# Expert tiles of 128 rows, all expert weights resident in SBUF, results in two regions by tile parity

## The chip, the cores and the metric

The kernel runs on one core of one Trainium2 chip. The metric is device time in microseconds (us) of one execution, lower is better; a version's time is the median of its runs. A core has TensorE (PE, matmuls; its weight loads are shown as PEld), VectorE (DVE), ScalarE (ACT), GpSimd (POOL), SyncE (SP) and 16 DMA engines, which work side by side and wait for each other through semaphores. All tensors are float32.

## What is computed

Gated cross attention of 32 batches of 100 tokens over 1444 context rows, followed by a feed-forward part with 12 experts, of which each token uses three. Cut to what matters:

```
x = x + tanh(g_xattn) * attention(layernorm(x), ctx)          # 32 x 100 x 256
h = layernorm(x); logits = h @ Wr + br                        # 12 experts
top_vals, top_idx = top_k(softmax(logits), 3); ew = softmax(top_vals)
for e in range(12):
    sel = top_idx == e; mask = sel.any(-1); w_e = sum(ew where sel) / max(sel.sum(), 1)
    y = relu(h @ w1[e] + b1[e]) @ w2[e] + b2[e]               # 256 -> 640 -> 256
    out = out + mask * (w_e * y)
phi = sigmoid(relu(mean_tokens(out) @ Wp1 + bp1) @ Wp2 + bp2)
x = x + tanh(g_ffn) * out * (1 - 0.8 * (phi > 0.7))
```

So 9,600 pairs of a token and an expert go through an expert.

## The kernel before

The program has two blocks. The first, `attention`, takes some 1,760 us. It also routes: at the end of each batch POOL scatters the 100 normalised rows three times into the DRAM tensor `rows_by_expert` (`xs`), which has a region for each expert; a row there carries 256 values and, for each expert, the number of the row of `results_by_token` (`ys`) to which its result is to be added. When the last batch is done DVE makes a table in SBUF: for each tile its expert, its first row in `xs`, and the column of the weight. At the same time `clear_pads` on SP and ACT (L295) zeroes one tile's worth of rows behind each expert's last row, 12 DMAs, and SP waits for them (L400). During the last batch ACT issues one DMA that clears `ys` (L592).

The second block, `experts`, is what the change is about. `RT` is the rows of a tile, 256. The number of tiles is fixed: `TILES = (9600 + 12 * (RT - 1)) // RT` = 49. They are in order of expert, and tiles behind the last expert work on zeros. The matmuls of a tile of 256 rows are, each done as two passes, so two instructions in the profile:

- `transpose_x` (L1405): four transposes of the rows `x_t` into `xT_ps`.
- `h_ps` (L1424): 5 chunks of 128 hidden values, 2 matmuls each with a 128x128 piece of w1 as stationary operand and the tile's rows (`xT`, 256 columns) as the moving one: 20 instructions.
- `y_ps` (L1438): for each half of 128 rows 5 matmuls, the hidden values `hid` stationary and w2 (256 columns) moving: 20 instructions.

PE goes h of tile t, transposes of t+1, y of t-1. ACT does five Relu with the bias from PSUM to `hid` (L1300), then copies the next `xT` (L1285), then reads the expert's number from the table and loads the next b2, broadcast over the partitions (L1280). DVE works out the rows of the results (`places`, L1347 and L1353), multiplies b2 by the expert's weight (L1367) and, for each half, evicts `y_ps * weight + b2_w` to `y_t` (L1374). POOL scatters each half into `ys` with an indirect DMA that adds in DRAM (L1211). Rows without a token go to spare rows of their own. Because a token can be in tiles of three experts, POOL starts tile t only when tile t-1 has landed (`y_stored`); the two halves of a tile belong to one expert and are in flight together.

SP loads for every tile: the rows, four tiles deep (L1230), and w1, b1 and w2 of its expert, two tiles deep (L1238, L1242, L1246), 1.31 MB a tile whether or not the expert is the one of the tile before. Each reads the table first. A load into a buffer waits until that buffer's matmuls are done.

After the last tile SP reads `ys` back in 5 pieces of 640 KB (L1269). DVE adds rows within each piece (L1381, L1384), PE sums them by batch (L1449, L1453), a small chain gives the factor, and DVE and SP finish and store the output.

The rule that POOL follows:

```
if t > 1:
    pool.wait_ge(y_stored[(t - 2) % OUT], 16 * RB * ((t - 2) // OUT + 1))
for r in range(RB):
    pool.wait_ge(y_read, RB * (t - 1) + r + 1)
    pool.indirect_dma_start(
...
```

## Time and profile before

| | us |
|---|---|
| median of 3 runs | 2262.12 (2259.59 to 2262.18) |
| profiled execution | 2268.39 |
| its span | 2266.4 |
| PE busy | 2145.9 (95%) |
| DVE busy | 1411.2 (62%) |
| ACT busy | 1160.2 (51%) |
| POOL busy | 805.1 (36%) |
| mean DMA rate | 152 GB/s |

The span is the time between the first and the last recorded instruction; 2.0 us of the execution lie outside it. Busy time counts instructions of an engine, without its register, semaphore and DMA-issuing instructions. Times in the rows count from the start of the span. A matmul's record is longer than the distance to the next one, since matmuls overlap in the array: distances between starts tell the pace. "Landing" is the time from a DMA's issue to the last byte's receipt.

### The profile page before, as it was taken

The page shows a single profiled execution, that of the slowest core. Times are in us where ns is not written, and L with a number is a line of the kernel's source. Part 1 is how long each engine was busy: PE and PEld are TensorE (multiplying, and loading weights), DVE is VectorE, ACT ScalarE, POOL GpSimd, SP SyncE. Part 2 cuts the span into 40 slices and gives each one's busy share as a digit, 9 for nine tenths or more (in the row PEclk, how much of TensorE's full clock was granted, in tenths as well). Part 3 has the DMA queues.
Part 4 walks back from the last instruction along what each step waited for, and adds up shares of the span by engine and source line. Part 5 has one row for each costly group of instructions (what it writes and reads, how often), then busy time and mean ns, then how long its engine had stood idle before and what let it go on. Part 6 is the DMA issues. An engine that isn't in the chain of part 4 may idle for free. (4 is left out here: it accounts for less than half of the span.)

```text
span 2266.4 us, 61917 instructions
## 1 busy us (share of the span) xinstructions
PE 2145.9 (95%) x23554; PEld 1870.7 (83%) x23554; DVE 1411.2 (62%) x3223; ACT 1160.2 (51%) x2765; POOL 805.1 (36%) x1199
## 2 busy tenths in 40 slices
PE   5899999999999999999999999999995789999995
PEld 4688888888888888888888888888874678888884
DVE  4777777777777777777777777777763111111113
ACT  1366666666666666666566656666653223333331
POOL 4323433343344334333433443343311233333331
PEclk9999999999999999999999999999996899999997
DMA  5555555555555555555555555555532786887775
GB/s 135 148 137 148 137 137 140 134 136 144 137 133 134 139 143 140 139 140 134 134 143 137 136 133 137 148 136 139 130 107 58 207 266 187 221 222 218 213 213 169
DMA packets 253828, 345.07 MB, mean 152 GB/s; under 512 B 90296, under 2 KB 170652, under 8 KB 253404
## 3 DMA queue, kind: packets, MB, share of 16 engines
q1 hardware_dynamic: 221228, 303.28, 50.0%
q0 software_dynamic: 20256, 23.21, 5.4%
q10 hardware_dynamic: 12048, 14.63, 2.1%
q8 instruction: 186, 3.05, 0.6%
q14 instruction: 110, 0.90, 0.1%
HBM read 155.83 MB, written 42.86 MB: 88 GB/s over the span
## 5 line engine op out<-in xcount | busy, mean ns | idle before, releaser
L637 DVE TENSOR_REDUCE max_part<-max_ps 100x1 f32<-100x512 f32 (+1 forms) x1536 | 993.9, 655 | 355.1 <-PE max_ps L925 326.8
L513 ACT ACTIVATE probs<-score_ps 128x400 f32<-128x400 f32 x1498 | 733.4, 503 | 411.6 <-PE score_ps L908 402.9
L925 PE MATMUL max_ps<-k_stack,q_stack 96*100 96x512 f32 (+1 forms) x1536 | 597.4, 389 | 15.4 <-DVE max_part L637 14.9
L908 PE MATMUL score_ps<-q_stack,k_stack 97*128 97x200 f32 (+1 forms) x2996 | 599.2, 282 | 0.9
L908 PEld LDWEIGHTS score_ps<-q_stack,k_stack 97*128 97x128 f32 (+1 forms) x2996 | 464.2, 184 | 66.1 <-issue 30.4
L442 POOL TENSOR_TENSOR ctx_hi<-ctx_raw,zero_col 128x256 fp32r<-128x256 f32 (+1 forms) x384 | 213.6, 589 | 467.1 <-PE v_ps L939 433.7
L976 PE MATMUL pv_ps<-probs,v_ones 128*17 128x100 f32 x12288 | 304.9, 251 | 5.5 <-ACT pv_out L521 2.8
L976 PEld LDWEIGHTS pv_ps<-probs,v_ones 128*17 128x17 f32 x12288 | 257.5, 98 | 51.8 <-issue 39.0
L925 PEld LDWEIGHTS max_ps<-k_stack,q_stack 96*100 96x100 f32 x1536 | 257.2, 167 | 28.2 <-DVE max_part L637 23.6
L1300 ACT ACTIVATE hid<-h_ps,b_c 128x256 f32<-128x256 f32 x245 | 116.2, 474 | 311.0 <-PE h_ps L1424 305.2
L1211 POOL DMA_INDIRECT results_by_token<-y_t,slot x98 | 152.6, 1557 | 317.5 <-DVE y_t L1374 183.3
L447 POOL TENSOR_TENSOR ctx_lo<-ctx_raw,ctx_hi 128x256 fp32r<-128x256 f32 (+1 forms) x384 | 257.7, 703 | 7.5
L1374 DVE SCALAR_TENSOR_TENSOR y_t<-y_ps,wexp,b_w 128x256 f32<-128x256 f32 x98 | 47.4, 484 | 318.6 <-PE y_ps L1438 318.6
L562 ACT ACTIVATE k_hl<-k_ps,bk_c 128x512 fp32r<-128x512 f32 (+1 forms) x192 | 127.2, 663 | 221.0 <-PE k_ps L956 196.6
L1424 PE MATMUL h_ps<-xT,w_raw 128*128 128x256 f32 x980 | 225.3, 386 | 10.9 <-DMA w_raw<-in_w 9.9
L939 PE MATMUL v_ps<-w_hi,ctx_hi 128*128 128x256 f32 (+1 forms) x768 | 219.3, 286 | 10.5 <-ACT v_ones L573 10.5
L1424 PEld LDWEIGHTS h_ps<-xT,w_raw 128*128 128x128 f32 x980 | 187.7, 193 | 42.3 <-DMA w_raw<-in_w 15.7
L1438 PE MATMUL y_ps<-w_raw,hid 128*128 128x256 f32 x980 | 219.5, 379 | 0.0
L939 PE MATMUL v_ps<-w_hi,ctx_lo 128*128 128x256 f32 (+1 forms) x768 | 216.7, 282 | 0.0
L939 PE MATMUL v_ps<-w_lo,ctx_hi 128*128 128x256 f32 (+1 forms) x768 | 216.4, 282 | 0.0
L1438 PEld LDWEIGHTS y_ps<-w_raw,hid 128*128 128x128 f32 x980 | 182.5, 190 | 22.9
L939 PEld LDWEIGHTS v_ps<-w_lo,ctx_hi 128*128 128x128 f32 (+1 forms) x768 | 142.5, 186 | 28.2
(192 smaller groups left out, 2351.3 us busy)
## 6 DMA issues: line engine op xcount, KB each, us to landing
k_stack<-k_hl SPq DMA_DIRECT2D x512, 128.0 KB, 2.6
w_raw<-in_w SPq DMA_DIRECT2D x98, 640.0 KB, 6.0
ctx_raw<-in_ctxT SPq DMA_DIRECT2D x64, 512.0 KB, 4.5
k_stack<-k_hl SPq DMA_DIRECT2D x512, 64.0 KB, 2.2
k_stack<-k_hl SPq DMA_DIRECT2D x256, 105.0 KB, 2.4
ctx_raw<-in_ctxT SPq DMA_DIRECT2D x32, 420.0 KB, 4.8
k_stack<-k_hl SPq DMA_DIRECT2D x256, 52.5 KB, 2.0
x_t<-rows_by_expert SPq DMA_DIRECT2D x49, 269.0 KB
```

Of the source, the lines that this page charges most:

```text
L442: ins = pool.tensor_tensor(ctx_hi[:, c % 2, k, cols], ctx_raw[:, k, cols], zero[:].broadcast_to([128, CW[j] // 2]), ALU.add)
L447: ins = pool.tensor_tensor(ctx_lo[:, c % 2, k, cols], ctx_raw[:, k, cols], ctx_hi[:, c % 2, k, cols].bitcast(F32), ALU.subtract)
L513: act.activation(probs[0:tw, n % PROBS, :], score_bank(n)[0:tw, 0:UH * SQ], ACT.Exp, scale=SCALE).then_inc(exp_done, 1)
L562: act.activation(k_hl[:, o, 1, 0:CW[j]], k_ps[:, 0:CW[j]], ACT.Identity, bias=bk_c[:, o:o + 1]).then_inc(k_hi_ready, 1)
L637: dve.tensor_reduce(max_part[b % 2][:, h, j:j + 1], max_ps[m % 2][0:SQ, 0:CW[j]], AX.X, ALU.max).then_inc(max_read, 1)
L908: ins = pe.matmul(score_bank(n)[0:TW[i], 2 * SQ * p:2 * SQ * (p + 1)], k_stack[b % 2][:, 2 * u + p, 128 * i:128 * i + TW[i]], q_stack[b % ...
L925: pe.matmul(max_ps[m % 2][0:SQ, 0:CW[j]], q_stack[b % 3][0:96, h // 2, SQ * (h % 2):SQ * (h % 2) + SQ], k_stack[b % 2][0:96, h // 2, k0[j] ...
L939: ins = pe.matmul(v_ps[0:tw, 0:D], c[:, (NC * b + i // TPC) % 2, k, keys], w[:, 1, k, :], start=(k == 0 and p == 0), stop=(k == KD - 1 and ...
L976: ins = pe.matmul(pv_ps[32 * h:32 * h + VW, u * SQ:u * SQ + SQ], v_ones[b % 2][:, i, UH * u + h, :], probs[:, n % PROBS, h * SQ:h * SQ + S ...
L1211: pool.indirect_dma_start(out=ys, out_offset=bass.IndirectOffsetOnAxis(ap=slot[(t - 1) % AHEAD][:, r:r + 1], axis=0), in_=y_t[(t - 1) % OU ...
L1424: ins = pe.matmul(h_ps[c][:, 0:RT], w1_raw[par][:, k, 128 * c:128 * c + 128], xT[:, k, :], start=(k == 0), stop=(k == KD - 1))
L1438: ins = pe.matmul(y_ps[r][:, 0:D], hid[other][:, m, rows], w2_raw[other][:, m, :], start=(m == 0), stop=(m == FM - 1))
```

## The change

A tile has 128 rows, and there are (9600 + 12 * 127) // 128 = 86 of them. The table, the spare rows and `clear_pads` follow from `RT`. SP loads the 12 experts' w1, b1 and w2 once into `w_all` (123 KB of each partition), expert t at the time of tile t for the first tiles, with the rows of four tiles ahead between them. For each tile ACT copies w1 and b1 of its expert from `w_all` into one of two buffers (1285 columns), two tiles ahead, and DVE copies w2 (1280 columns), one tile ahead. The first 12 copies on each engine wait for the load of expert t (`loaded_for`); for this each expert gets at least one tile. b2 is loaded once for all experts and multiplied once by the weights. `ys` has two regions of 3,200 rows; a tile adds to the one of its parity, and POOL starts tile t when tile t-2 has landed. At the end both regions are read back and added. ACT clears the second region with a DMA of its own ten tile steps after the first. In `attention`, `heads` shares the memory of `x1`, and DVE waits for the store of the last `x1` two steps earlier. The x1 load for the end moves from ACT at tile 8 to SP at tile 12.

```diff
-RT = 256
+RT = 128
+RESULTS = 2
...
-                if g == NT * B:
+                if g in (NT * B, NT * B + 10):
...
-                    act.dma_start(results, zero_rows[:, 0:D]...
+                    act.dma_start(results[g > NT * B], zero_rows[:, 0:D]...
...
+            step(dve.tensor_scalar(ntiles, ntiles, 1.0, None, ALU.max))
...
+            for t in range(TILES):
+
+                stored_by(pool, t - RESULTS)
+                pool.wait_ge(y_read, t + 1)
+                pool.indirect_dma_start(
+                    out=ys, out_offset=bass.IndirectOffsetOnAxis(ap=slot[t % SLOTBUFS][:], axis=0),
+                    in_=y_t[t % OUT][:], in_offset=None,
+                    compute_op=ALU.add).then_inc(y_stored[t % OUT], 16)
...
+            def load_weights(e):
+                sp.dma_start(w_all[:, e, 0:KD * FF].rearrange("p (k f) -> p k f", k=KD), w1[e]).then_inc(w_in[e], 16)
+                sp.dma_start(w_all[:, e, KD * FF:WX], b1[e]).then_inc(w_in[e], 16)
+                sp.dma_start(w_all[:, e, WX:WW].rearrange("p (m d) -> p m d", m=FM), w2[e]).then_inc(w_in[e], 16)
+
+            for t in range(AHEAD - 1):
+                load_rows(t)
+                load_weights(t)
+            for t in range(TILES):
+                if t + AHEAD - 1 < NE:
+                    load_weights(t + AHEAD - 1)
+                if on(t + AHEAD - 1):
+                    load_rows(t + AHEAD - 1)
...
+            def copy_w1(t):
                 expert = act.value_load(table[0:1, bass.ds(t, 1)], min_val=0, max_val=NE - 1)
+
+                loaded_for(act, t)
+                wait(act, h_done, FM * (t - 1))
+                act.activation(w1_c[t % 2][:], w_all[:, bass.ds(expert, 1), 0:WX].rearrange("p o w -> p (o w)"),
+                               ACT.Copy).then_inc(w1_ready, 1)
...
+            act.dma_start(b2_w[:, 0:NE, :], b2.partition_broadcast(128)).then_inc(b2_in, 16)
             x_copy(0)
+            copy_w1(0)
+            copy_w1(1)
+            for t in range(TILES):
+                for c in range(FM):
...
                 if on(t + 1):
...
                     x_copy(t + 1)
...
+                if on(t + 2):
+
+                    act.wait_ge(h_relu, FM * (t + 1))
+                    copy_w1(t + 2)
...
+            for t in range(TILES + 1):
                 if on(t + 1):
                     places(t + 1)
                 if on(t - 1):
...
+                    dve.scalar_tensor_tensor(
+                        y_t[(t - 1) % OUT][:], y_ps[(t - 1) % 2][:, 0:D], wexp[:, bass.ds(column[t - 1], 1)],
...
+                if on(t + 1):
+                    copy_w2(t + 1)
             for i in range(PARTS):
+                dve.tensor_tensor(res[0][:, pieces[i], :], res[0][:, pieces[i], :], res[1][:, pieces[i], :],
+                                  ALU.add).then_inc(res_added, 1)
```

On PE, where a turn in the middle of the expert stage stood as follows before (`h_ps` the hidden chunks, `xT_ps` the transposes, `y_ps` the result; the last figures are the output's size, x4 four alike; each of these rows is two instructions in the profile but for the transposes):

```order
L1424 MATMUL h_ps3<-xT,w1_raw0 128x256 [waits h_relu]
L1424 MATMUL h_ps3<-xT,w1_raw0 128x256
L1424 MATMUL h_ps4<-xT,w1_raw0 128x256 [waits h_relu]
L1424 MATMUL h_ps4<-xT,w1_raw0 128x256
L1410 MATMUL xT_ps<-ident2,x_t1 128x128 [waits xT_ready,x_in1]
L1410 MATMUL xT_ps<-ident2,x_t1 128x128 x3
L1438 MATMUL y_ps0<-w2_raw1,hid1 128x256 [waits y_read,h_relu,w2_in1]
L1438 MATMUL y_ps0<-w2_raw1,hid1 128x256 x4
L1438 MATMUL y_ps1<-w2_raw1,hid1 128x256 [waits y_read]
L1438 MATMUL y_ps1<-w2_raw1,hid1 128x256 x4
```

and stands now:

```order
L1416 MATMUL h_ps3<-xT,w1_c0 128x128
L1416 MATMUL h_ps4<-xT,w1_c0 128x128 [waits h_relu]
L1416 MATMUL h_ps4<-xT,w1_c0 128x128
L1404 MATMUL xT_ps<-ident2,x_t0 128x128 [waits xT_ready,x_in0]
L1404 MATMUL xT_ps<-ident2,x_t0 128x128
L1427 MATMUL y_ps1<-w2_c1,hid1 128x256 [waits y_read,h_relu,w2_ready]
L1427 MATMUL y_ps1<-w2_c1,hid1 128x256 x4
L1416 MATMUL h_ps0<-xT,w1_c1 128x128 [waits h_relu,xT_ready,w1_ready]
L1416 MATMUL h_ps0<-xT,w1_c1 128x128
```

The same number of h matmuls for a tile has half the columns, one group of y matmuls is gone, and what PE waits for is a copy's semaphore (`w1_ready`, `w2_ready`) instead of a DMA's.

On ACT the same turn before (TENSOR_LOAD reads the table, ISA are register instructions, the last row is the b2 load):

```order
L1300 ACTIVATE hid1<-h_ps3,b1_c1 128x256 [waits h_done]
L1300 ACTIVATE hid1<-h_ps4,b1_c1 128x256 [waits h_done]
L1285 ACTIVATE xT<-xT_ps 128x512 [waits h_done,xT_done]
L1279 TENSOR_LOAD table [waits b2_w_ready]
L1279 ISA x2
L1280 ISA
L1280 DMA b2_b0<-in_b2 128x256
```

and now:

```order
L1293 ACTIVATE hid0<-h_ps3,w1_c0 128x128 [waits h_done]
L1293 ACTIVATE hid0<-h_ps4,w1_c0 128x128 [waits h_done]
L1279 ACTIVATE xT<-xT_ps 128x256 [waits h_done,xT_done]
L1268 TENSOR_LOAD table [waits h_relu]
L1268 ISA x2
L1272 ISA [waits h_done]
L1272 ACTIVATE w1_c0<-w_all 128x1285
L1293 ACTIVATE hid1<-h_ps0,w1_c1 128x128 [waits y_done,w1_ready,h_done]
```

A copy of 1285 columns stands in the place of the b2 load, ahead of the next tile's first Relu.

## Rows read from the trace of the kernel before

**Rows 1.** The chain that ended last, expert stage: start us, us, what
```profile
1770.11 6.93 PE h_ps L1424 x20
...
1806.06 4.32 PE h_ps L1424 x20
...
1815.13 4.50 PE h_ps L1424 x20
...
2217.51 4.58 PE h_ps L1424 x20
```
**Rows 2.** Busy time by stretch; at the end granted clock, DMA share, GB/s
```profile
1770.00:1775.00 5.00, 4.89 (x12) 3.93 (x13) 0.32 (x2) 0.95 (x2) 0.00 (x0) 0.51 1.01 401
...
1800.00:2200.00 400.00, 392.54 (x1885) 342.02 (x1884) 71.65 (x213) 124.78 (x257) 131.39 (x86) 0.99 0.79 221
```
**Rows 3.** PE: short matmuls (timeline), transposes (chain), weight loads (the page's groups)
```profile
1026.31 1.03 PE L998 MATMUL small_ps<-xT_q,w_qo 128*128 128x100 f32 x8
...
1027.12 0.45 PE L908 MATMUL score_ps<-q_stack,k_stack 97*128 97x200 f32 x2
...
1846.86 0.44 PE xT_ps L1410 x4
...
L1424 PEld LDWEIGHTS h_ps<-xT,w_raw 128*128 128x128 f32 x980 | 187.7, 193 | 42.3 <-DMA w_raw<-in_w 15.7
```
**Rows 4.** ACT: groups (busy us, mean ns), and one turn of the timeline
```profile
L1300 ACT ACTIVATE hid<-h_ps,b_c 128x256 f32<-128x256 f32 x245 | 116.2, 474 | 311.0 <-PE h_ps L1424 305.2 <-issue 5.8
L1285 ACT ACTIVATE xT<-xT_ps 128x512 f32<-128x512 f32 x49 | 29.3, 597 | 26.1 <-PE xT_ps L1410 26.1
...
L526 ACT ACTIVATE xT_q<-small_ps 128x200 f32<-128x200 f32 x32 | 10.6, 332 | 4.5 <-PE small_ps L991 4.5
...
1900.89 0.60 ACT L1285 ACTIVATE xT<-xT_ps 128x512 f32<-128x512 f32 x1
1901.62 0.35 ACTq L1280 DMA_DIRECT2D b_b<-in_b  x1
```
**Rows 5.** DVE: groups, eviction of y and an SBUF operation of 588 columns
```profile
L1374 DVE SCALAR_TENSOR_TENSOR y_t<-y_ps,wexp,b_w 128x256 f32<-128x256 f32 x98 | 47.4, 484 | 318.6 <-PE y_ps L1438 318.6
...
L870 DVE TENSOR_TENSOR probs<-probs,ctx_raw 128x588 f32<-128x588 f32 x1 | 0.8, 771 | 0.0
```
**Rows 6.** POOL's scatters: durations ns and landing min/median/max; the last one's landing (chain)
```profile
L1211 POOL DMA_INDIRECT results_by_token<-y_t,slot x98: 1552/1555/1644, 1786.8 to 2233.9; - x98
...
DMA to landing us min/median/max: 3.6/6.5/10.7
...
2233.86 3.85 DMA results_by_token<-y_t,slot
```
**Rows 7.** DMA queues from 1800 to 2200: packets, MB, share of the engines
```profile
q1 hardware_dynamic: 30128, 67.68, 52.7%
q0 software_dynamic: 12384, 11.28, 19.0%
```
**Rows 8.** Timeline: the first instruction of SP in the expert block
```profile
1763.91 0.42 SPq L1230 DMA_DIRECT2D x_t<-rows_by_expert  x1
```
**Rows 9.** The clearing DMAs: SP's wait for the last, and landing of all
```profile
SPq L401 <- DMA rows_by_expert<-ctx_raw: 7.4, 1, 7.4
...
DMA to landing us min/median/max: 3.8/6.7/7.7
```
**Rows 10.** Timeline of the end, from the last eviction to the pooled sums
```profile
2230.76 0.48 DVE L1374 SCALAR_TENSOR_TENSOR y_t<-y_ps,wexp,b_w 128x256 f32<-128x256 f32 x1 [1.58 <-PE y_ps L1438]
...
2237.73 2.66 SPq L1269 DMA_DIRECT2D res<-results_by_token  x5
2241.75 0.69 DVE L1381 TENSOR_TENSOR pair_sum<-res 128x512 f32<-128x512 f32 x1 [10.51 <-DMA res<-results_by_token]
...
2248.05 0.69 DVE L1381 TENSOR_TENSOR pair_sum<-res 128x512 f32<-128x512 f32 x1 [0.42 <-DMA res<-results_by_token]
...
2250.88 0.22 ACT L1316 ACTIVATE pooled<-h_ps 128x64 f32<-128x64 f32 x1 [28.18 <-PE h_ps L1453]
```

More of the change, by code:

```diff
@@ L286, in attention @@
         N_TAIL = 4
-        results = ys[1:1 + SLOTS, :].rearrange("(p i) d -> p i d", p=128)
+        results = [ys[1 + SLOTS * k:1 + SLOTS * (k + 1), :].rearrange("(p i) d -> p i d", p=128)
+                   for k in range(RESULTS)]
         def clear_pads(eng, some):
@@ L1113, in experts @@
         h_ps = [pb(f"h_ps{c}", [128, 512]) for c in range(FM)]
-        y_ps = [pb(f"y_ps{r}", [128, 512]) for r in range(RB)]
+        y_ps = [pb(f"y_ps{p}", [128, 512]) for p in range(2)]
         consts = sem("consts")
@@ L1118, in experts @@
         x_in = [sem(f"x_in{p}") for p in range(AHEAD)]
-        w1_in = [sem(f"w1_in{p}") for p in range(2)]
-        w2_in = [sem(f"w2_in{p}") for p in range(2)]
-        b1_in = [sem(f"b1_in{p}") for p in range(2)]
-        b2_in = [sem(f"b2_in{p}") for p in range(2)]
+        w_in = [sem(f"w_in{e}") for e in range(NE)]
+        w1_ready = sem("w1_ready")
+        w2_ready = sem("w2_ready")
+        b2_in = sem("b2_in")
         xT_done = sem("xT_done")
@@ L1158, in experts, with stored_by, loaded_for @@
         pieces = [slice(TPP // PARTS * i, TPP // PARTS * (i + 1)) for i in range(PARTS)]
-        results = [ys[1 + B * SQ * k:1 + B * SQ * (k + 1), :].rearrange("(p i) d -> p i d", i=TPP)
-                   for k in range(COPIES)]
-        def turns(eng, turn):
-            for t in range(TILES + 1):
-                turn(t, t % 2, t // 2)
+        results = [ys[1 + SLOTS * k:1 + SLOTS * (k + 1), :].rearrange("(p i) d -> p i d", i=TPP)
+                   for k in range(RESULTS)]
         def on(t):
             return 0 <= t < TILES
-        def nth(s, par, d=0):
-            return s + (par + d) // 2 + 1
+        def stored_by(eng, t):
+            if t >= 0:
+                eng.wait_ge(y_stored[t % OUT], 16 * (t // OUT + 1))
+        def loaded_for(eng, t):
+            if t < NE:
+                eng.wait_ge(w_in[t], 16 * 3)
         block = ctx.enter_context(nc.Block())
@@ L1248, in turn @@
-            def turn(t, par, s):
+                sp.dma_start(x_t[t % AHEAD][:], xs[bass.ds(row, RT), :]).then_inc(x_in[t % AHEAD], 16)
+            def load_weights(e):
[5 more added lines that the diff above has]
+                load_weights(t)
@@ L1429, in turn @@
                 if on(t - 1):
-                    other = 1 - par
-                    wait(pe, w2_in[other], 16 * nth(s, par, -1))
-                    wait(pe, h_relu, FM * t)
-                    for r in range(RB):
-                        wait(pe, y_read, RB * (t - 2) + r + 1)
-                        rows = slice(128 * r, 128 * r + 128)
-                        for m in range(FM):
-                            ins = pe.matmul(y_ps[r][:, 0:D], hid[other][:, m, rows], w2_raw[other][:, m, :],
-                                            start=(m == 0), stop=(m == FM - 1))
-                        ins.then_inc(y_done, 1)
-            turns(pe, turn)
+                    pe.wait_ge(w2_ready, t)
+                    pe.wait_ge(h_relu, FM * t)
+                    wait(pe, y_read, t - 2)
+                    for m in range(FM):
+                        ins = pe.matmul(y_ps[(t - 1) % 2][:, 0:D], hid[(t - 1) % 2][:, m, :], w2_c[(t - 1) % 2][:, m, :],
+                                        start=(m == 0), stop=(m == FM - 1))
+                    ins.then_inc(y_done, 1)
             pe.wait_ge(masks, 2)
```

217 lines of the change are left out of this document (88 added, 129 removed).

## The prediction

> **What bounds the kernel now.** I read the chain of waits first. From 1770 us on it is PE almost alone: a tile's h matmuls take 4.32 us, the chain then runs through transposes and y matmuls, and from one tile's h to the next are 1815.13 - 1806.06 = 9.07 us [rows 1]. In the stretch 1800 to 2200 PE is busy 392.5 of 400 us at a granted clock of 0.99, the 2.4 GHz level [rows 2]. From the first h to the last, 48 turns, pass 2217.51 - 1770.11 = 447.4 us [rows 1]. 48 times 9.07 less the first turn's missing y (4.32) would be 431; the other 16 us are waits for weights and the first microseconds at 0.51 of the clock [rows 2]. So the expert stage, 1763.9 to 2237, is a PE stage, and what counts is PE time per tile times tiles, as long as ACT, DVE, POOL and the DMA engines keep pace. The attention stage ahead of it is hardly touched.
>
> **PE per tile.** A turn before has 20 instructions of h (4.32), four transposes (0.44) and 20 of y (9.07 - 4.32 - 0.44 = 4.31), so 0.216 us for each one with 256 columns. Now y has 10 with 256 columns: 2.16. Transposes are two: 0.44 / 4 = 0.11 each, 0.22. The open price is h: 20 instructions with 128 moving columns, each with a 128x128 weight load. Lower bound: half of the columns, half of 0.216 = 0.108. Upper bound: the weight load's own record, 0.193 [rows 3]. Nearest rows: the 8 instructions of the query projection, 128x128 stationary and 100 moving columns, start at 1026.31 and the next matmul starts at 1027.12, 0.10 each [rows 3]; and the transposes, 128 columns with a 128x128 load each, 0.11 [rows 3]. I take 0.108: h costs 2.16. **A turn costs 2.16 + 0.22 + 2.16 = 4.54 us.** For 86 tiles that is 390 us against 49 times 9.07 = 444: the rows fall from 12,544 to 11,008.
>
> **ACT per tile.** 512 columns of Copy take 0.597 and 200 columns 0.332 [rows 4]: 0.85 ns a column and 0.16 fixed. Relu with a bias takes 0.474 at 256 columns [rows 4], so 0.365 at 128, five make 1.83. The xT copy of 256 columns: 0.38. The read of the table: in the timeline 0.73 pass from the start of the xT copy to the b2 DMA behind it [rows 4]; I count 0.75 from the xT copy's start, with the copy inside. The copy of w1 is not in the trace. Lower bound 0.60 (the 512 column copy), upper bound five activations of 256 columns, 2.37; by the line above 1285 columns give 1.25, and I take that. Sum 1.83 + 0.75 + 1.25 = 3.83, under 4.54. It also fits in order: the fifth Relu ends some 2.8 us after the turn's first h, the xT copy starts then, the w1 copy ends at 2.83 + 0.75 + 1.25 = 4.8, and the next tile's first h chunk is ready at 4.54 + 0.7 = 5.2. PE hides the copy with 0.4 us to spare.
>
> **DVE, POOL, SP per tile.** DVE has the eviction, 0.484 [rows 5], two small operations and a table read (about 1 us with their gaps), another table read (0.7), and the w2 copy. Its dearest bound is one column per cycle as in the 588 column row, 0.771 [rows 5], so 1280 columns give 1.5; the cheapest is nothing below half of that. Sum at most 3.7: under 4.54, and w2 is wanted a turn later. POOL: one scatter of 1.56 us a turn [rows 6], as before in 9.07 us two. Its wait for tile t-2: two turns, 9.08 us, must hold landing, 6.5 in the median, 10.7 at worst [rows 6], plus 0.7 of issue. The DMA engines' load falls: before, the hardware queue took 52.7% of them [rows 7], nearly all of it weights; now a turn moves 0.14 MB of rows and one scatter. The last landing with the engines free took 3.85 [rows 6]. So POOL waits for nothing. SP issues one load a turn. The waits for weights inside the steady stage, most of the 16 us, go, and nothing takes their place but the first 12 loads.
>
> **The first 12 tiles.** ACT's copy for tile t+2 waits for expert t+2 and stands ahead of the Relu of t+1, so no tile passes far beyond the loads. The row and weight loads run at 67.68 MB / (0.527 x 400 us) = 321 GB/s [rows 7] up to 401 in the best 5 us [rows 2]; I take 361. An expert with a tile's rows is 1.45 MB, 4.0 us; once scatters run, each adds 0.190 x 400 / 86 = 0.88 [rows 7], 4.9. From the first row load: expert 0 with b2 (12 rows broadcast, 1.57 MB) is 3.0 MB, 8.2 us, and some 2.2 to get going: 10.4. Expert 3 at 22.5, expert 11 at 22.5 + 8 x 4.9 = 61.6. Its copy, five Relu, the xT copy and latencies make 3.8: tile 11's h starts at 65.4. PE alone would be there at about 60 to 64, so this costs little. Bounds: 4.5 a tile (PE's own pace), 62; 5.4 (the 321 GB/s), 69.
>
> **The sum**, against the profiled execution (span 2266.4, run 2268.39). (1) Clearing halves to 128 rows an expert. SP waits 7.4 us for the last [rows 9]; with half the bytes the shortest landing, 3.8 [rows 9], applies, and the barrier follows: -4.0 (bounds -6.5, if half of the 13 us at full DMA load goes, and -1). DVE's table grows by some 2.7 us of work on 86 instead of 49 tiles but ends before that. (2) The second clearing of results is one more issue of 0.6 us on ACT while the last batch drains and the DMA engines are idle: +0.3 (0 to 0.6). The moved wait and the shared buffer: nothing, since the store is a batch old. (3) From the first row load, 1763.91 [rows 8], to the end of the last eviction, 2231.24 [rows 10]: before 467.3. Now 65.4 + 74 turns x 4.54 = 401.4 to tile 85's h, then h, y(84), y(85), 6.5, and 0.8 to the end of the eviction: 408.7. -58.6. (4) From there to the last landing before 6.5 us, since POOL was a scatter behind [rows 10]; now 0.75 + 3.85: -1.9. (5) Reading back: before, pieces arrive each (2248.05 - 2241.75) / 4 = 1.58 us, the first 4.0 after its issue, and the pooled sums start at +13.15 [rows 10]. Now each piece is a pair, 3.15 us, so the last is there at 4.0 + 1.58 + 4 x 3.15 = 18.2; behind it stand the addition of 1280 columns (1.5), the two old ones (1.15) and PE's last four (1.1): 22.1. +8.9. The rest is unchanged. **Sum -55.3**: span 2211.1, run 2213.1. The profiled run lay 6.3 above the median of 2262.12, so the forecast for the median is 2206.8.
>
> **Two rules of the Trainium skill.** The skill's page "TensorE: Matmul & The Clock Gate", Back-to-back issue gap, says that in a stream of weight loads and matmuls 128 columns pace at about 81 ns where the isolated gap would be 56. By that ratio, applied to 0.107, an h instruction would be 0.155 and the turn 5.48, an estimate from that page: the first rival below in a milder form, some 2277. The trace does not agree in the float32 rows nearest to it, 0.10 and 0.11. The skill's page "SBUF — State Buffer", Who interferes with whom, says that a float32 SBUF copy on DVE holds the port pair that GpSimd needs, and an indirect DMA's descriptors wait for its end. No row before has the two side by side; by this rule a scatter is late by up to the copy.
>
> **The rivals.** *Weight loads pace h (slower than before).* If each of the 20 h instructions has to wait out its weight load's record, 0.19, a turn costs 3.8 + 0.22 + 2.16 = 6.18: 74 x 1.64 = +121, 2328. It decides from 0.145 per instruction, where 20 x 0.037 x 74 eats the 55 us. Against it: the 0.10 and 0.11 of [rows 3]. Four in a hundred. *The scatters of two tiles overtake PE's pace (slower).* DVE's copy and POOL's scatter begin at the same time, 0.7 us after the eviction. If the copy (up to 1.5) delays the scatter and landing stays at its worst, 10.7 [rows 6], two turns take 12.9, a turn 6.45: +141, 2348; from a landing of 8.3 POOL leads, from 9.8 the gain is gone. Against it: 3.85 with engines free. Four in a hundred. *ACT sets the pace.* If the w1 copy costs like five activations (2.37), ACT needs 4.95 a turn, 5.3 if the table read doesn't overlap the xT copy: +30 to +57, 2237 to 2264, no change at the far end. For it: only 0.7 us of room and a copy that no row shows. Ten in a hundred. *The first tiles are slow.* If loads run at the mean 221 GB/s of the stage [rows 2], or PE, waiting at each tile, stays at the 1.2 GHz level while they come, an expert takes 6.6 to 7.5 or a turn 9.1: +25 to +40, 2232 to 2247. For it: the clock was at 0.51 in the first turn [rows 2]. Against: PE needs 4.5 of every 4.9 us. Eight in a hundred.
>
> **How the numbers follow.** The forecast holds 74 in 100, with its own range 2192 to 2232: h between 0.10 and 0.118 (-12 to +15), first tiles -3 to +4, clearing and read-back -6 to +6. The range for 8 in 10 takes in the slow first tiles and part of the ACT case: 2192 to 2246. A measurement can tell 0.2%, 4.5 us, from no change. Faster: forecast, slow first tiles and most of the ACT case, 0.89; same 0.02; slower 0.09.
>
> **What would show it.** In the profile after: h groups of 20 in 2.16 us and 4.54 from h to h; ACT idle before each tile's first Relu, released by PE; the w1 copy at 1.25 us; POOL released by DVE and not by its own landings after tile 15; tile 11's h at 62 to 69 us from the first row load; the pooled sums 22 us after the read-back's issue. The forecast is wrong if h's pace is over 0.12, if Relus start without idle time, or if POOL's waits are for landings.

## The result, and the profile after

| | before | after |
|---|---|---|
| median of 4 runs, us | 2261.38 | 2209.23 |
| ratio, 95% interval | | 0.9762 (0.9747 to 0.9778) |
| profiled execution, its span | 2268.39, 2266.4 | 2204.03, 2202.3 |
| PE, DVE, ACT, POOL busy | 2145.9, 1411.2, 1160.2, 805.1 | 2086.9, 1480.1, 1305.6, 806.0 |
| mean DMA rate, GB/s | 152 | 133 |

The kernel before has one run more here than in the table further up. The change takes 52.2 us off the medians; 2206.8 was forecast. The spans of the two profiled executions differ by 64.1, more than the medians, since the one of before lay above its median and the one of after below. A stretch of the profile that leaves that scatter out is used below: from SP's first row load to the pooled sums. It was 2250.88 - 1763.91 = 487.0 [rows 8, 10] and is 2186.79 - 1748.50 = 438.3, 48.7 less.

Windows of the profile after, busy us of PE, PEld, DVE, ACT, POOL, then granted clock, DMA share, GB/s (to be read beside [rows 2]):

```profile
1756.00:1760.00 4.00, 0.06 (x1) 0.00 (x0) 1.28 (x2) 1.66 (x2) 0.00 (x0) 0.50 1.03 404
1768.00:1792.00 24.00, 24.00 (x166) 22.58 (x166) 8.16 (x20) 17.59 (x40) 8.52 (x5) 1.00 1.06 381
...
1800.00:2100.00 300.00, 300.00 (x2085) 283.20 (x2084) 106.13 (x261) 220.34 (x457) 117.32 (x66) 1.00 0.37 74
```

PE has no gap left in 300 us, at a granted clock of 1.00, the 2.4 GHz level. The DMA engines' share is 0.37 where it was 0.79 [rows 2]. One turn, PE (start us, us; beside [rows 1]):

```profile
1963.60 2.39 PE L1416 MATMUL h_ps<-xT,w_c 128*128 128x128 f32 x20
1965.83 0.38 PE L1404 MATMUL xT_ps<-ident,x_t 128*128 128x128 f32 x2
1966.05 2.32 PE L1427 MATMUL y_ps<-w_c,hid 128*128 128x256 f32 x10
1968.21 2.39 PE L1416 MATMUL h_ps<-xT,w_c 128*128 128x128 f32 x20
```

The starts give h 2.23, transposes 0.22, y 2.16, and 4.61 from h to h. The other engines in that turn, in brackets the idle time and its releaser (beside [rows 4 to 6]):

```profile
1964.04 0.48 DVE L1364 SCALAR_TENSOR_TENSOR y_t<-y_ps,wexp,b_w 128x256 f32<-128x256 f32 x1 [2.38 <-PE y_ps L1427]
1964.24 2.15 ACT L1293 ACTIVATE hid<-h_ps,w_c 128x128 f32<-128x128 f32 x5 [0.52 <-PE h_ps L1416]
1964.82 0.83 DVE L1344 COPY w_c<-w_all 128x1280 f32 x1 [0.29 <-issue]
1965.27 1.81 POOL L1213 DMA_INDIRECT results_by_token<-y_t,slot  x1 [2.81 <-DVE y_t L1364]
...
1966.29 0.38 ACT L1279 ACTIVATE xT<-xT_ps 128x256 f32<-128x256 f32 x1
1967.06 1.28 ACT L1272 ACTIVATE w_c<-w_all 128x1285 f32 x1 [0.40 <-issue]
```

ACT, DVE and POOL all wait for PE or for what comes from PE. Both copies are hidden; the w1 copy takes 1.28, the w2 copy 0.83. Between 1900 and 2100 the scatters' landings took 3.9 to 4.9, median 4.1. POOL's waits, by releaser, from 1800 to 2100:

```profile
POOL results_by_token L1213 <- DVE y_t L1364: 173.3, 62, 2.8
...
POOL results_by_token L1213 <- DMA results_by_token<-y_t,slot: 8.3, 2, 5.5
```

The first tiles in the timeline (beside [rows 8] and the first row of [rows 1]). The row load leads, then ACT's copy of w1, released by the loads, and PE:

```profile
1748.50 0.38 SPq L1229 DMA_DIRECT2D x_t<-rows_by_expert  x1
...
1758.69 1.28 ACT L1272 ACTIVATE w_c<-w_all 128x1285 f32 x1 [2.21 <-DMA w_all<-in_w]
...
1760.02 4.47 PE L1416 MATMUL h_ps<-xT,w_c 128*128 128x128 f32 x20 [3.96 <-ACT w_c L1272]
...
1762.36 1.28 ACT L1272 ACTIVATE w_c<-w_all 128x1285 f32 x1 [2.39 <-DMA w_all<-in_w]
...
1765.29 2.47 PE L1416 MATMUL h_ps<-xT,w_c 128*128 128x128 f32 x20 [0.58 <-issue]
...
1765.96 1.28 ACT L1272 ACTIVATE w_c<-w_all 128x1285 f32 x1 [0.76 <-DMA w_all<-in_w]
```

The first three experts are copied 3.7 and 3.6 us apart, each as soon as it has landed, faster than PE works through tiles (4.61). And the end (beside [rows 10]): last eviction, read-back, the first and the last addition of the two regions.

```profile
2159.59 0.48 DVE L1364 SCALAR_TENSOR_TENSOR y_t<-y_ps,wexp,b_w 128x256 f32<-128x256 f32 x1 [1.67 <-PE y_ps L1427]
...
2164.86 5.00 SPq L1258 DMA_DIRECT2D w_all<-results_by_token  x10
2170.25 1.49 DVE L1373 TENSOR_TENSOR w_all<-w_all 128x1280 f32<-128x1280 f32 x1 [10.17 <-DMA w_all<-results_by_token]
...
2182.96 1.49 DVE L1373 TENSOR_TENSOR w_all<-w_all 128x1280 f32<-128x1280 f32 x1 [0.46 <-DMA w_all<-results_by_token]
```

### The profile page after: what moved, and what is told of

Read it like the earlier page. It is cut to its first block and busy times, and to the rows that moved or that the text cites. A ratio compares the mean times of both kernels' runs of the same rounds, so it can differ in the third digit from the quotient of the medians.

```text
span 2202.3 us, 63899 instructions
## 1 busy us (share of the span) xinstructions
PE 2086.9 (95%) x24150; PEld 1848.7 (84%) x24150; DVE 1480.1 (67%) x3330; ACT 1305.6 (59%) x3073; POOL 806.0 (37%) x1187
## 5 line engine op out<-in xcount | busy, mean ns | idle before, releaser
L930 PE MATMUL max_ps<-k_stack,q_stack 96*100 96x512 f32 (+1 forms) x1536 | 597.2, 389 | 12.8 <-DVE max_part L641 12.5
L1416 PEld LDWEIGHTS h_ps<-xT,w_c 128*128 128x128 f32 x1720 | 207.4, 193 | 9.5 <-ACT w_c L1272 4.4
L1416 PE MATMUL h_ps<-xT,w_c 128*128 128x128 f32 x1720 | 208.0, 277 | 4.5 <-ACT w_c L1272 4.0
L1427 PE MATMUL y_ps<-w_c,hid 128*128 128x256 f32 x860 | 199.7, 379 | 0.0
L1293 ACT ACTIVATE hid<-h_ps,w_c 128x128 f32<-128x128 f32 x430 | 156.8, 367 | 69.2 <-PE h_ps L1416 42.1
L1364 DVE SCALAR_TENSOR_TENSOR y_t<-y_ps,wexp,b_w 128x256 f32<-128x256 f32 x86 | 41.6, 484 | 224.6 <-PE y_ps L1427 222.0
L1427 PEld LDWEIGHTS y_ps<-w_c,hid 128*128 128x128 f32 x860 | 156.8, 190 | 17.8
L577 ACT ACTIVATE v_ones<-v_ps 128x256 f32<-128x256 f32 (+1 forms) x384 | 146.6, 382 | 33.9 <-PE v_ps L944 20.2
```

What stands on the lines that cost most here:

```text
L930: pe.matmul(max_ps[m % 2][0:SQ, 0:CW[j]], q_stack[b % 3][0:96, h // 2, SQ * (h % 2):SQ * (h % 2) + SQ], k_stack[b % 2][0:96, h // 2, k0[j] ...
L1293: act.activation(hid[t % 2][:, c, :], h_ps[c][:, 0:RT], ACT.Relu, bias=w1_c[t % 2][:, KD * FF + c:KD * FF + c + 1]).then_inc(h_relu, 1)
L1416: ins = pe.matmul(h_ps[c][:, 0:RT], w1_c[t % 2][:, k * FF + 128 * c:k * FF + 128 * c + 128], xT[:, k, :], start=(k == 0), stop=(k == KD - 1))
L1427: ins = pe.matmul(y_ps[(t - 1) % 2][:, 0:D], hid[(t - 1) % 2][:, m, :], w2_c[(t - 1) % 2][:, m, :], start=(m == 0), stop=(m == FM - 1))
```

## The experiments

The theory behind the forecast: PE is the bound before and after; fewer rows and no waits for weights give the gain; resident weights and the second region are what lets the small tiles run at PE's pace; the copies hide. The rivals: the rows alone do it; the second region is not needed; ACT is near its limit. The experiments ran on three chips, each with the kernel before beside them. The chips differ (2248, 2265 and 2247 us for the kernel before), so ratios are compared across chips and times within one.

**Tiles of 128 rows alone, and with two regions.** Weights are streamed as before. The edit of the first is `RT`, room in the tables, and the shared buffer of `attention`; of the second, in addition:

```diff
-                    if t > 1:
-                        pool.wait_ge(y_stored[(t - 2) % OUT], ...)
+                    if t > 2:
+                        pool.wait_ge(y_stored[(t - 3) % OUT], ...)
...
-COPIES, PARTS, TPP = 1, 5
+COPIES, PARTS, TPP = 2, 5
```

> The kernel before with tiles of 128 rows and nothing else of the change: weights still streamed for each tile (now 86 x 1.31 MB), one region of results, POOL still starts a tile when the one before it has landed (the buffers of the routing part are shared as in the change, to make room). The PE work per tile is that of the change, a turn of 4.61. Theory A, both other parts are needed: a turn moves 1.31 MB of weights, 0.13 of rows and 0.26 by the scatter, 1.7 MB, at 313 to 401 GB/s 4.3 to 5.4 us, and the scatters form a chain of landing (3.7 to 6.5) plus up to 0.75 of issue, 4.1 to 7.2 a tile: some 2230 to 2400, most likely slower than the kernel before (2261), with POOL's waits for its own landings or PE's waits for w_raw as the largest. Theory B, the gain is the smaller number of rows and the rest is ornament: turns of 4.6 to 4.7, 2195 to 2210, since the read-back of one region saves 8.8.

> As tile128, with the two regions of results added, weights still streamed. Theory A: POOL's chain is out of the way, the loads are left: a turn of 4.7 to 5.4 us, 2215 to 2275, PE's waits before h and y released by w_raw. Theory B, loads hide: 4.61 a turn, 2205 to 2212, as the changed kernel. Over tile128 by more than 10 us tells that the scatters' chain, not the loads, set the pace there.

Measured: 2408.66, ratio 1.0703 (1.0678 to 1.0728), and 2412.68, ratio 1.0729 (1.0711 to 1.0747). Small tiles with streamed weights are 160 us slower than the kernel before. Theory B falls, and the second region saves nothing here. PE's h groups in the timeline of the first:

```profile
1954.72 4.10 PE L1424 MATMUL h_ps<-xT,w_raw 128*128 128x128 f32 x20 [2.72 <-DMA w_raw<-in_w]
1961.03 2.39 PE L1424 MATMUL h_ps<-xT,w_raw 128*128 128x128 f32 x20
1970.32 4.63 PE L1424 MATMUL h_ps<-xT,w_raw 128*128 128x128 f32 x20 [4.52 <-DMA w_raw<-in_w]
```

The windows of the same kernel (columns as above), and SP's own waits from 1800 to 2200 (us in total, times, longest):

```profile
1961.00:1963.40 2.40, 2.40 (x23) 2.40 (x23) 1.01 (x4) 1.47 (x4) 0.81 (x1) 1.00 0.63 149
...
1970.40:1974.80 4.40, 4.40 (x21) 4.40 (x22) 0.51 (x2) 1.47 (x4) 1.55 (x1) 0.50 0.86 251
...
1800.00:2200.00 400.00, 304.60 (x1723) 279.50 (x1722) 68.44 (x216) 114.63 (x324) 83.90 (x54) 0.85 0.81 239
...
SPq L1246 <- PE y_ps L1438: 214.7, 53, 11.1
```

Every second turn waits for a weight load (29 waits in 54 turns), 2.7 and 4.5 us in these rows, and the h behind the wait runs wholly or mostly at the 1.2 GHz level (granted clock 0.50 in the window above): its record is 4.6 or 4.1 us where it is 2.4 otherwise. From the first h to the last 2369.57 - 1744.41 = 625.2 us pass, 7.35 a turn. Of these PE is busy 304.6 / 400 x 7.35 = 5.60 and idle 1.75. Without stalls it is busy 4.61, so the slower matmuls add 1.0 to the 1.75, and a stall is paid about one and a half times.

My expectation had 4.3 to 5.4 us for the loads, the turn's 1.7 MB at 313 to 401 GB/s, and that was too low. It took the DMA engines as always full. The mixture of loads does not rule that out: in the kernel after, expert loads, row loads and five scatters together ran at 381 GB/s and a share of 1.06 (1768 to 1792, above). Here the share is 0.81 at 239 GB/s, close to the 0.79 and 221 of before [rows 2], and the loads are held back: w2 of tile t+2 waits on SP for y of t, and rows and w1 of t+3 stand behind it. SP waited so in 53 of 54 turns, 4.0 us each. An estimate from these rows: at a share of 1.06 the same bytes would move at 239 x 1.06 / 0.81 = 313 GB/s, and a turn's 95.4 MB / 54.4 = 1.75 MB would take 5.6 us. So the engines' work alone would have kept the turn above 4.61. That the rest, up to 7.35, lies in the waits for free buffers and the slow matmuls behind them is argued from these rows, not shown: no run had deeper buffers with streamed weights. The changed kernel has them too (five for the rows, four for `y_t`, six for `slot`) and loads b2 once; no run takes these apart from the resident weights.

**256 rows without loading weights.** SP loads w1, b1 and w2 for tiles 0 and 1 only:

```diff
             def load_weights(t, par):
+                if t >= 2:
+                    return
```

> The kernel before, tiles of 256 rows, without the loads of w1, b1 and w2 from the third tile on: all tiles use the weights of the first two (this part of the computation is left out). It gives the most that resident weights could bring with 256 rows, without any copies. Theory A (my sum): 16 us of the 48 turns were waits for weights and the slow first microseconds; without loads the part behind the first two turns goes, -8 to -12, 2249 to 2253; the gain of the change is then mostly in the rows. Rival: weights are hidden with 256 rows and the waits move elsewhere, within 3 us of the kernel before. A third: the loads slow the rest of the DMA work too (row loads, scatters), -16 or more.

Measured: 2235.31 against 2248.11, ratio 0.9944 (0.9928 to 0.9961), 12.8 less. In its timeline h starts at 1748.72 for the first and 2183.00 for the last tile, 434.3 us instead of 447.4 [rows 1]:

```profile
1956.19 4.48 PE L1426 MATMUL h_ps<-xT,w_raw 128*128 128x256 f32 x20
1960.50 0.60 PE L1412 MATMUL xT_ps<-ident,x_t 128*128 128x128 f32 x4
1960.94 4.48 PE L1440 MATMUL y_ps<-w_raw,hid 128*128 128x256 f32 x20
1965.26 4.48 PE L1426 MATMUL h_ps<-xT,w_raw 128*128 128x256 f32 x20
```

PE has no idle time from the second tile's h on. This shows how the gain between first and last h divides: 447.4 - 434.3 = 13.1 us are waits for weights, and 434.3 - 392.6 (after, 1760.02 to 2152.61) = 41.7 are the smaller number of rows. At most 13 us can be had from resident weights with the old tile. The rows are the larger part, but with the weights streamed two tiles deep they were not to be had, as the two kernels above show.

**One region.** The changed kernel with `RESULTS = 1`, so that POOL waits for tile t-1 and one region is read back; run on two chips, the second time beside the changed kernel itself.

> The changed kernel with one region of results: POOL starts tile t when tile t-1 has landed, and the read-back is of one region. The read-back is 8.8 us shorter. Theory A (the second region pays): the chain of a scatter is its landing, 4.1 in the median and 8.0 at worst, and up to 0.75 from the landing to the next issue, 4.8 to 5.1 against a turn of 4.61: 0.2 to 0.5 times 86 less 8.8, 2217 to 2245, with POOL's waits for own landings in most turns. Theory B (it doesn't): the 4.1 are counted from the issue and nothing much stands between landing and issue, a chain of 4.1 to 4.4, hidden under 4.61, and the time is 2200, 9 less than the changed kernel.

> The changed kernel once more, unchanged, on the chip of the next three, so that their differences to it are on one chip: ratio to the kernel before 0.976. It also shows how far the attention stage, which the change leaves alone but for one wait, varies between profiles (first row load at 1748.5 in the one profile so far, and at 1736 to 1742 in the four of the first experiments on another chip).

> The changed kernel with one region of results, beside the changed kernel on one chip. From the profile of the first run: the 86 tiles take as long (392.6 and 393.6 from first h to last), POOL's chain of landing and issue (4.0 to 4.6) keeps PE's pace of 4.61 but ends two tiles behind, which costs 10.5 instead of 4.8 from the last eviction to the read-back, and the read-back is 8.8 shorter. Theory A, the second region pays nothing: -2 +- 2 against after_again. Theory B, by the ratios of the two chips (0.9771 and 0.9762) it pays some 2: +2.

Measured: 2196.62, ratio 0.9771 (0.9755 to 0.9788), on the first chip. On the second 2210.24 (0.9753) beside 2211.12 (0.9769) for the changed kernel: no difference that these runs can tell. From the first row load to the pooled sums the profiles of one region have 436.3 and 440.2 us, those of the changed kernel 438.3 and 438.8. So the second region pays nothing that can be measured, and of my two first theories neither had the mechanism right: I had the chain as too slow, or as hidden. The timeline of the first profile shows both halves. In the middle:

```profile
1962.73 0.83 DVE L1344 COPY w_c<-w_all 128x1280 f32 x1 [0.29 <-issue]
1962.84 2.14 POOL L1213 DMA_INDIRECT results_by_token<-y_t,slot  x1 [2.47 <-DMA results_by_token<-y_t,slot]
...
1967.34 0.83 DVE L1344 COPY w_c<-w_all 128x1280 f32 x1 [0.29 <-issue]
1967.47 2.12 POOL L1213 DMA_INDIRECT results_by_token<-y_t,slot  x1 [2.49 <-DMA results_by_token<-y_t,slot]
```

and at the end, last eviction, POOL's last scatters, read-back, pooled sums:

```profile
2148.29 0.48 DVE L1364 SCALAR_TENSOR_TENSOR y_t<-y_ps,wexp,b_w 128x256 f32<-128x256 f32 x1 [1.67 <-PE y_ps L1424]
2151.29 1.55 POOL L1213 DMA_INDIRECT results_by_token<-y_t,slot  x1 [2.56 <-DMA results_by_token<-y_t,slot]
2155.32 1.55 POOL L1213 DMA_INDIRECT results_by_token<-y_t,slot  x1 [2.48 <-DMA results_by_token<-y_t,slot]
2159.27 2.52 SPq L1258 DMA_DIRECT2D w_all<-results_by_token  x5
...
2172.35 0.22 ACT L1304 ACTIVATE pooled<-h_ps 128x64 f32<-128x64 f32 x1 [28.16 <-PE h_ps L1437]
```

POOL is released by its own landings throughout. From one scatter to the next are 4.5 to 4.7 us where DVE's copy begins shortly before it (2.0 to 2.15 of them on POOL), 4.2 to 4.4 where the copy begins 0.88 after it (1.80 on POOL), and 4.0 to 4.2 where the two don't meet (1.55). PE doesn't notice (393.6 us from first h to last, after 392.6), since four buffers of `y_t` and six of `slot` stand between them. DVE does, in part: 27 times, 50 us in all, it waits for the landing of the scatter that last used its `slot`. POOL falls behind twice: while the experts load (waits of 6.3 to 6.4 us for a landing) and beside the 3.2 MB load of x1 (one wait of 9.4, until 1814). After that it gains little: from 1814.08 to 2155.32 there are 77 scatters, 4.43 each on average against PE's 4.61, seven of them 5.4 to 6.3. What makes those seven long is not shown; there are some without the w2 copy too. Two tiles' scatters (three in the second profile) are still to come after the last eviction. So the last eviction is followed by 10.5 us until the read-back (after: 4.8; in the second profile 14.4), and the pooled sums come 13.1 behind that (after: 21.9). So 8.8 are saved at the read-back and 5.7 to 9.6 lost ahead of it.

**One region, w2 copied for two tiles only.** DVE copies nothing from the third tile on:

```diff
-                if on(t + 1):
+                if on(t + 1) and t == 0:
                     copy_w2(t + 1)
```

> one_region with DVE's copies of w2 left out from the third tile on (all tiles use the w2 of the first two experts; that part of the computation is left out). In one_region_again POOL's scatter took 2.0 to 2.2 us and its chain 4.61 a tile while DVE copied, and 1.55 and 3.98 in the last tiles, where it didn't. Theory A (the copy makes the scatter long): 1.55 us and 4.0 a tile throughout, POOL catches up with PE after the expert loads and then waits for DVE's y_t, the last eviction to the read-back is 4.8 instead of 10.5 to 14.9, and the time is 0.970 to 0.973 of the kernel before, 6 to 10 less than one_region. Rival: the chain in the middle is 4.61 because PE paces it, POOL's waits stay with its own landings, the same time as one_region (0.975 to 0.977).

Measured: 2186.73 against 2247.18, ratio 0.9725 (0.9710 to 0.9740). That is 6 to 10 us below one region's 0.9753 and 0.9771, and its interval ends below that of the changed kernel. From the first row load to the pooled sums the profile has 431.7 us, 4.6 and 8.5 less than the two of one region. POOL's scatters, durations in ns, min/median/max, from 1780 us on:

```profile
L1213 POOL DMA_INDIRECT results_by_token<-y_t,slot x83: 1551/1555/1573, 1785.3 to 2152.2; - x83
```

In one_region_again the same row from 1800 us on reads 1552/1792/2098. Without the copy POOL catches up sooner, but slowly: its first 26 scatters behind the x1 load take 4.12 us each on average, where one_region's take 4.36. Between 1800 and 2100 its waits are still for landings, 67 of 68, but the scatters at 2134.61, 2139.22 and 2143.83 are released by DVE's `y_t`, and the read-back is issued 6.6 us after the last eviction (2149.15 + 0.48 to 2156.21). Theory A holds, but not in its "throughout" and not in its 4.8 us to the read-back. So with one region the w2 copy costs some 5 to 10 us. What the second region buys is cover for that copy and for the slow first landings.

**Two copies of w1 on ACT.** A second copy of 1285 columns for each tile, into a buffer that nobody reads:

```diff
                 wait(act, h_done, FM * (t - 1))
+                act.activation(w1_twice[:], w_all[:, bass.ds(expert, 1), 0:WX]...
                 act.activation(w1_c[t % 2][:], w_all[:, bass.ds(expert, 1), 0:WX]...
```

> The changed kernel with a second copy of w1 and b1 on ACT for each tile, into a buffer that nobody reads. It shows how much room ACT has. From the trace after: five Relu in 2.15, the xT copy 0.38, issue 0.39, the copy 1.28 and 0.51 idle make the turn of 4.61. Theory A (the sum): 1.28 and some 0.05 to 0.1 more than fit into 0.51 of slack, and the Relus run closer: a turn of 5.2 to 5.4, +50 to +65 on 2210, 0.998 to 1.006 of the kernel before. That would be the point of the rival that ACT sets the pace. Rival B: a copy lies two tiles ahead, so PE is not held by it: within 5 of the changed kernel. In a third case PE's gaps bring the granted clock down as with streamed weights (0.86), +80 or more.

Measured: 2194.34, ratio 0.976 (0.9745 to 0.9775), that of the changed kernel. Theory A is refuted: 50 to 65 us were expected and nothing came. ACT in the timeline:

```profile
1963.44 1.26 ACT L1277 ACTIVATE w_c<-w_all 128x1285 f32 x1
1964.61 1.60 ACT L1298 ACTIVATE hid<-h_ps,w_c 128x128 f32<-128x128 f32 x5
1966.11 0.38 ACT L1284 ACTIVATE xT<-xT_ps 128x256 f32<-128x256 f32 x1
1966.88 1.28 ACT L1274 ACTIVATE w_twice<-w_all 128x1285 f32 x1 [0.40 <-issue]
1968.06 1.26 ACT L1277 ACTIVATE w_c<-w_all 128x1285 f32 x1
1969.22 0.35 ACT L1298 ACTIVATE hid<-h_ps,w_c 128x128 f32<-128x128 f32 x1
```

The turn is 1969.22 - 1964.61 = 4.61 still. My sum took the five Relus at the 2.15 us they have after the change. But most of that is waiting for h chunks: starting later, the five take 1.50 from the first one's start to the start of the xT copy. And an activation starts about 0.1 before the record of the one ahead ends (1963.44 + 1.26 = 1964.70 against 1964.61, and 1966.88 + 1.28 = 1968.16 against 1968.06), so that two copies cost 2.34, not 2.54. ACT's only idle time in these rows is the 0.40 of issue ahead of the copies. Little can be left: the five Relus took 1.24 at the least elsewhere (early_rows_first, 1750.72 to 1751.96), so by an estimate from these rows 0.3 us at most. A third copy was not tried.

**The clearing at 256 rows again.**

```diff
-    REGION = B * SQ + RT
+    REGION = B * SQ + 256
...
-                eng.dma_start(xs[bass.ds(row, RT), :]...
+                eng.dma_start(xs[bass.ds(row, 256), :]...
```

> The changed kernel with the clearing behind each expert as before, 256 rows instead of 128 (12 DMAs of twice the bytes). My term for the halved clearing was -4.0 (bounds -6.5 and -1); the two profiles showed 17.3 and 11.7 us from the first clearing DMA to the first row load, -5.7. Theory A: +4 to +6 against the changed kernel, 0.978 to 0.9795 of the kernel before, with 8.8 instead of 6.7 us for the issues. Rival: the table on DVE now takes 37 more tiles and ends just before, so that the clearing isn't what is waited for: +0 to +2.

Measured: 2199.65, ratio 0.9779 (0.9766 to 0.9792). The changed kernel itself did not run on that chip. Beside it ran two_w1_copies, whose ratio is that of the changed kernel: clear256 is 5.3 above it by medians and 4 by ratios. The intervals of the ratios overlap a little, but its lowest time is above the highest of two_w1_copies. SP in the timeline of clear256:

```profile
1728.84 8.96 SPq L299 DMA_DIRECT2D rows_by_expert<-ctx_raw  x6
1745.16 0.40 SPq L1229 DMA_DIRECT2D x_t<-rows_by_expert  x1
```

and of the kernel after:

```profile
1736.83 6.66 SPq L299 DMA_DIRECT2D rows_by_expert<-ctx_raw  x6
1748.50 0.38 SPq L1229 DMA_DIRECT2D x_t<-rows_by_expert  x1
```

16.3 against 11.7 us from the first clearing DMA to the first row load. The other profiles bear that out: 16.4 and 17.3 in the two more that clear 256 rows, 10.9 to 12.1 in all eleven that clear 128. The halved clearing is worth 4.6 by this pair and 4.2 to 6.4 by all, as theory A had it, and the times agree.

**An earlier start.** After the change PE's first h came 11.5 us after the first row load, because rows, w1 and w2 of the first experts and b2 of all were in flight together and ACT's copy waited for w1, b1 and w2. The edits of early_start:

```diff
-                eng.wait_ge(w_in[t], 16 * 3)
+                eng.wait_ge(w1_in[t], 32) if w1 else eng.wait_ge(w_in[t], 16)
...
-            act.dma_start(b2_w[:, 0:NE, :], b2.partition_broadcast(128)).then_inc(b2_in, 16)
             x_copy(0)
             copy_w1(0)
+            act.dma_start(b2_w[:, 0:NE, :], b2.partition_broadcast(128)).then_inc(b2_in, 16)
```

and b2's multiplication moves from ahead of DVE's first turn to behind it. early_one_region has `RESULTS = 1` as well. early_rows_first loads the rows of four tiles and w1 of expert 0 before all else, issues b2's load after the second copy, and multiplies just before the first eviction.

> The changed kernel with three edits at the start of the expert stage: each expert's w1 and b1 have a semaphore of their own and ACT's copy waits for these alone, not for w2; the load of b2 for all experts (1.5 MB) is issued after the first w1 copy, not ahead of the first rows; and its multiplication by the weights goes on DVE behind the first turn. Theory A: the first h came 11.5 us after the first row load because rows, w1, w2 and b2 (2.9 MB) were all in flight and the copy waited for the last; with 0.8 MB it comes after 6 to 8, and since experts land 3.6 us apart, faster than PE's 4.61, the gain stays: -3 to -5.5 against after_again. Rival: the clock is at the 1.2 GHz level when PE begins, the first tiles' loads become the bound instead, and the gain is under 1.5.

> Both: the earlier start and one region of results. If the two add: -5 to -7.5 against after_again, 0.974 or less of the kernel before. Rival: with an earlier start more scatters fall into the time of the twelve expert loads, where landings were up to 10, POOL falls further behind and DVE waits for its slots: no better than early_start.

> early_start with three edits more: SP loads the rows of tiles 0 to 3 and w1 of expert 0 before all other weights; b2's load comes after the second w1 copy; and its multiplication stands just before the first eviction. In early_start the first h came 6.3 us after the first row load instead of 11.7, but tile 2's h waited 2.0 us for rows and w1 that came behind b2's 1.5 MB, so that the last h was only 2.4 earlier, 402.0 after the first row load, not 404.3. Theory A: the order of the loads took the rest; last h at 398.5 to 400, 4 to 6 less than the changed kernel, 0.9745 or less. Rival: the total bytes of the first twelve experts decide, something else is late by as much, and it stays at 402.

Measured: early_start 2206.41, ratio 0.975 (0.9734 to 0.9766), beside 0.9769 (0.9755 to 0.9783) of the changed kernel: 4.7 less by medians, with intervals that overlap. early_one_region 2211.46, ratio 0.9769, no gain. early_rows_first 2192.93 on another chip, ratio 0.9752 (0.9738 to 0.9765), no better than early_start. PE of early_start:

```profile
1757.50 4.63 PE L1418 MATMUL h_ps<-xT,w_c 128*128 128x128 f32 x20 [3.42 <-ACT w_c L1273]
1763.08 2.47 PE L1418 MATMUL h_ps<-xT,w_c 128*128 128x128 f32 x20 [0.52 <-issue]
1770.55 2.47 PE L1418 MATMUL h_ps<-xT,w_c 128*128 128x128 f32 x20 [2.02 <-ACT xT L1280]
```

Counted from the row load (1751.24) the first h is 5.3 earlier, and the third tile gives 2.8 back: its w1 and rows land behind b2's 1.5 MB, ACT's copy of w1 for tile 2 starts at 1767.62, and in ACT's order the Relus of tile 1 stand behind it. In early_rows_first the second h starts at 1752.47, 14.6 after the row load, having waited for w1 of expert 1 (copied at 1749.54), and the last h is 404.1 after the row load, as in the changed kernel (404.1 and 404.4); in early_start it is 402.0. In early_one_region the second tile's h waited 5.7 and then took 4.4 us instead of 2.5. So theory A of these runs held for the first tile only. What is moved forward pushes another load back, and since ACT's copies stand ahead of Relus, whichever of them is late holds PE. Of the 5.3 us 2.1 stay.

## Why the prediction was right, and where its steps were off

| step | forecast | measured |
|---|---|---|
| clearing and second clearing | -3.7 | -4.6 (clear256 and after), -5.7 (before and after) |
| h instruction; turn | 0.108; 4.54 | 0.1115; 4.61 |
| tile 11's h from the first row load | 65.4 | 63.0 |
| row load to end of last eviction | 408.7 (-58.6) | 411.6 (-55.8) |
| last eviction to read-back | -1.9 | 6.49 to 4.79, -1.7 |
| read-back to pooled sums | +8.9 | 13.15 to 21.93, +8.8 |
| sum | -55.3 | -53.3 to -54.4 by these terms, -52.2 by the medians |

**PE's price, the largest term, was right.** The turn is 2.23 + 0.22 + 2.16. The query projection and the transposes [rows 3] were the right rows for 128 moving columns with a weight load each. The rival at 0.19 an instruction is refuted: the LDWEIGHTS records of h are 193 ns on average in both kernels, yet h instructions start 2.23 / 20 = 0.1115 us apart. From 128 to 256 columns an instruction goes from 0.1115 to 0.216 us, 0.82 ns or two cycles of 2.4 GHz a column, so I count it as two passes over its columns, 55.8 ns each at 128. The Trainium skill's "TensorE: Matmul & The Clock Gate", Back-to-back issue gap, gives 81 ns per matmul at 128 columns in a stream of loads and matmuls. The trace does not bear that out for these float32 instructions, neither as 81 ns a pass nor as the 0.155 an instruction that I had estimated from it. It agrees with the section "Wait — 56ns, not 53.3ns?" of the same page, which states 128 columns / 2.4 GHz and some 2.5 ns more. A turn took 0.07 us more than forecast, 5.2 us over the 74 turns that the sum counts.

**The first tiles: right in size, wrong in mechanism.** I let the loads pace tiles 0 to 11, at 361 GB/s and with 4.9 us each. They came at 381 to 404, 3.6 us apart, and from tile 2 on PE ran at its own 4.61. The first h came after 11.5 us, then 5.3 and 4.7 for two turns, nine of 4.61: 63.0. That is 2.4 less than forecast and takes back part of the 5.2, so that the stretch to the last eviction came out 2.9 over. This part of the closeness is luck: two errors of opposite sign.

**The waits for weights** were called most of 16 us; the run without loads shows 13.1.

**ACT as the bound** got ten in a hundred, from a sum of 3.83 with 0.7 us of room, and a price of +30 to +57 with a copy of 2.37. In two_w1_copies the two copies took 2.34 from start to start, as much as the 2.37 of that bound, and nothing was lost. What was off is the adding up of durations: the Relus' 1.83 were right as five times one (0.367 measured), but back to back they took 1.50, since one begins before the record of the one ahead ends. The room was at least the 1.16 of a second copy, not 0.7.

**POOL's two tiles.** The rule of the Trainium skill that I cited, "SBUF — State Buffer", Who interferes with whom, says that the engine that comes second to the shared ports is blocked until the first one's instruction ends. The trace agrees where the copy comes first. After: the copy ends at 1965.65, 0.38 after the scatter's start, and the scatter takes 1.81 instead of 1.555, 0.25 more. One region: overlaps of 0.72 and 0.70, 0.58 and 0.57 more. Each is the overlap less 0.13, within 0.01; the 0.13 is measured, not explained. It does not fit the simple form of the rule that a scatter is also 0.24 longer where the copy begins 0.88 after it (one_region, 1814 to 1875), while the copy keeps its 0.83. In the changed kernel all this costs nothing, since POOL has two turns of 4.61. The median landing fell from 6.5 to 4.1, at a DMA share of 0.37 instead of 0.79. The rival needed 8.3 in turn after turn, and 8.0 was the longest single one. What the forecast left out is a question that it did not need for its number: I costed what the second region adds, 8.8 us, and never what the kernel would lose without it. By the runs that is 5.7 to 9.6 us at the end of the stage and nothing on PE.

**The clearing** was -4.0 with bounds -6.5 and -1, and it is -4.6 by clear256, -4.2 to -6.4 by all profiles. The profiles alone would have misled: the first row load came 15.4 us earlier. But the clearing itself began 1746.57 - 1736.83 = 9.7 us earlier. Over the twelve later profiles its start lay between 1724 and 1744, and on one chip it was 1725.19 with the old attention part (tile256_weights_of_two) and 1724.25 to 1728.05 in the three kernels with the new one. So most of that part is spread between executions and chips, not the shared buffer or the moved wait, and the forecast rightly had nothing for it. The second clearing was not measured by itself.

What stays open: how far streamed weights at 128 rows would come with deeper buffers, what makes single scatters take 5.4 to 6.3 us with one region, and the 1 to 2 us between the sum of the terms and the medians, which is less than the interval of the ratio (0.16% of 2261 us, 3.5, to either side).

## What to carry to other kernels

Price a smaller tile first by the time of its operands, not of its matmuls: the same change of tile was +160 us with streamed weights and -52 with resident ones, and a stalled TensorE pays again through its clock. For an engine off the path, ask what it does back to back, not what the durations of its instructions add up to; the sum told of 0.7 us of room where at least 1.16 was there. And cost a second buffer against the kernel without it: here the second region gave at the end of the stage (5.7 to 9.6 us) what it took at the read-back (8.8).

## What the runs showed of the hardware

- In tile128 stalls of PE of 2.7 and 4.5 us were followed by h groups of 4.1 and 4.6 us instead of 2.4, the second at a granted clock of 0.50, the 1.2 GHz level.
- A DVE copy of 1280 float32 columns in SBUF takes 0.83 us and lengthens a scatter's record on POOL that begins beside it, by their overlap less 0.13: up to 2.14 us instead of 1.555. Where its own landings set POOL's pace, the scatter's period goes from 4.0 to 4.2 us up to 4.5 to 4.7. Without the copy all of 83 scatters took 1.55 to 1.57.
- Successive activations on ACT overlap by about 0.1 us in their records; five Relus of 0.367 took 1.50.
- Loads of 640 KB with row loads and scatters moved 381 GB/s at a DMA share of 1.06 when SP issued them ahead, and 239 at 0.81 when SP waited 4.0 us a turn for a free buffer.
